# First stage of a two-layer kernel: k and v from one 512-column product, q from a 256-column one, and v copied ahead of q

## The reference, cut to what matters

```python
Q = _linear(query, Wq, bq)   # 16 heads of 16 features; query = layernorm(x)
K = _linear(key, Wk, bk)     # key = value = ctx
V = _linear(value, Wv, bv)
Qf = jnp.fft.rfft(Q, axis=2)
Kf = jnp.fft.rfft(K, axis=2)
corr = jnp.fft.irfft(Qf * jnp.conj(Kf), n=Lx, axis=2)
corr_mean = corr.mean(axis=-1)
top_w, top_idx = jax.lax.top_k(corr_mean, 4)
# softmax over the four, then V rolled by the four lags and summed
...
x = x + out @ Wo.T + bo
```

## Time and profile before

| | |
|---|---|
| device time, three executions | 984.47, 981.14, 981.69 us |
| their median | 981.69 us |
| span of the profiled execution, first to last instruction | 979.1 us |
| median less that span | 2.6 us |
| PE matmul busy / weight loads busy | 846.7 us (86%) / 544.5 us (56%) |
| DVE / ACT / POOL busy | 697.8 (71%) / 529.5 (54%) / 304.3 us (31%) |
| mean granted TensorE clock | 0.947 |

### The profile page before, as it was taken

How to read it: one execution, slowest core, us unless ns; L and a number is a source line. 1 busy time by engine, 2 the same in 40 slices (tenths; PEclk the granted TensorE clock), 3 DMA queues, 4 the chain that set the end, 5 groups by cost and what they waited for, 6 DMA issues and landing times.

```text
span 979.1 us, 13076 instructions
## 1 busy us (share of the span) xinstructions
PE 846.7 (86%) x4559; PEld 544.5 (56%) x4559; DVE 697.8 (71%) x1256; ACT 529.5 (54%) x1004; POOL 304.3 (31%) x236
## 2 busy tenths in 40 slices
PE   3999989699999999989999888799998997008998
PEld 3776766578677887434444444444443443006887
DVE  2466677866766577679879999767765998895333
ACT  1444443555333566677666777133336995983432
POOL 2100000466311122578868888310002331000000
PEclk9999999899999999999989999989998999558999
DMA  8800000010000000000000000000001435830111
GB/s 286 273 1 1 1 1 1 0 55 1 1 1 12 1 1 1 1 1 1 2 1 1 2 1 2 1 0 1 0 1 43 172 150 192 354 120 21 44 54 55
DMA packets 23448, 45.44 MB, mean 46 GB/s; under 512 B 2323, under 2 KB 18646, under 8 KB 22230
## 3 DMA queue, kind: packets, MB, share of 16 engines
q1 hardware_dynamic: 21776, 43.08, 12.3%
q10 hardware_dynamic: 1606, 1.52, 0.5%
HBM read 27.80 MB, written 16.78 MB: 46 GB/s over the span
## 4 chain that ended last, share of the span: by engine, by line
PE 64%; DVE 13%; ACT 9%; POOL 7%; issue 4%; DMA 1%; ACTq 1%; DVEq 0%; SPq 0%; POOLq 0%
PE pair L1307 9%; PE pair L1354 8%; PE pair L985 5%; PE pair L1223 5%; POOL hat L608 4%; PE pair L1238 4%; PE pair L1093 3%; PE pair L1120 3%; PE pair L989 3%; DVE wide L1812 3%; PE pair L1199 2%; PE pair L1030 2%; PE pair L1122 2%; ACT upq L917 2%; ACT g2q L923 2%
## 5 line engine op out<-in xcount | busy, mean ns | idle before, releaser
L608 POOL TENSOR_TENSOR hat<-hat 128x1024 f32<-128x1024 f32 x62 | 145.4, 2360 | 38.1 <-DVE hat L1663 38.0
L1332 PE MATMUL pair<-xqs,wuT 128*128 128x512 f32 x192 | 85.5, 606 | 4.8 <-ACT up_stage L873 4.8
L1307 PE MATMUL pair<-xqs,wgT 128*128 128x512 f32 x192 | 84.5, 597 | 0.0
L1354 PE MATMUL pair<-wdT,hid 128*128 128x256 f32 x384 | 83.1, 379 | 0.3 <-DVE hid L1860 0.3
L525 POOL TENSOR_TENSOR rstd<-lnt,half 128x8 f32<-128x8 f32 (+2 forms) x15 | 26.5, 1767 | 170.0 <-DVE lnt L1398 170.0
L1354 PEld LDWEIGHTS pair<-wdT,hid 128*128 128x128 f32 x384 | 72.9, 190 | 11.0 <-DVE hid L1860 1.2
L1207 PE MATMUL pair<-rows,sel 32*128 32x512 bf16 x256 | 68.3, 395 | 9.9 <-ACT down_a L828 2.9
L1223 PE MATMUL pair<-hat,vz 128*32 128x128 f32 x1056 | 71.6, 282 | 2.8 <-DVE hat L1663 1.6
L1223 PEld LDWEIGHTS pair<-hat,vz 128*32 128x32 f32 x1056 | 53.8, 112 | 25.7 <-issue 23.3
L1332 PEld LDWEIGHTS pair<-xqs,wuT 128*128 128x128 f32 x192 | 37.2, 195 | 51.8 <-issue 51.8
L985 PE MATMUL pair<-wT,ft_sb 128*128 128x256 f32 x256 | 64.4, 395 | 0.0
(11 more groups left out here) (223 smaller groups left out, 1931.0 us busy)
## 6 DMA issues: line engine op xcount, KB each, us to landing
up_far<-up_stage SPq DMA_DIRECT2D x24, 512.0 KB, 2.6
ups<-up_far SPq DMA_DIRECT2D x8, 1536.0 KB, 6.8
x_sb<-in_x_dram SPq DMA_DIRECT2D x8, 512.0 KB, 7.8
c_sb<-in_ctx_dram SPq DMA_DIRECT2D x8, 512.0 KB, 8.2
out_dram<-x_sb SPq DMA_DIRECT2D x16, 256.0 KB, 2.1
four<-in_c_four_dram SPq DMA_DIRECT2D x1, 1280.0 KB, 6.3
deq<-in_L_ffn_w_gate_dram SPq DMA_DIRECT2D x1, 768.0 KB, 6.9
deq<-in_L_ffn_w_up_dram SPq DMA_DIRECT2D x1, 768.0 KB, 8.6
```

The costliest lines, as they stand in the source:

```text
L608: nc.gpsimd.tensor_tensor(hat[:, n % RING, :], hat[:, (n - 2) % RING, :], hat[:, n % RING, :], ALU.add).then_inc(summed, 1)
L1307: last = mm(bank[2 + oc][:], wgT[:, c, oc * 128:(oc + 1) * 128], xqs[:, s, c, :], start=(c == 0), stop=(c == DC - 1))
L1332: last = mm(bank[2 + oc], wuT[:, c, oc * 128:(oc + 1) * 128], xqs[:, t % 2, c, :], start=(c == 0), stop=(c == DC - 1))
L1354: last = mm(bank[s][:, 0:D], hid[:, s, ic, :], wdT[:, ic, :], start=(ic == 0), stop=(ic == IC - 1))
```

## The change

In `project`, the product of q stands alone in `bank[2 + s]` with a bias of 256 columns. k and v now share `bank[4 + s]`: a bias of 512 columns and two products of 512 columns, whose moving operand is `wT[:, 1:3, c, :]`, two runs of 256 columns. In `copy_qv` the copy of v comes first and the three copies of q behind it; each still waits for `proj_done`, and the semaphores are raised by the same copies as before. `products` reads k from `bank[4 + s]`. `fold_half` waits for `prod_done` of all batches beside `v_copied`.

```diff
@@ copy_qv (ACT)
+                nc.scalar.activation(vhat[:, at(b), :].rearrange("p o d -> p (o d)"), bank[4 + s][:, D:], ACT.Copy).then_inc(v_copied, 1)
                 q = bank[2 + s][:, 0:D]
                 nc.scalar.activation(qq[:, s, 0, :], q, ACT.Copy)
                 nc.scalar.activation(qq[0:64, s, 1, :], q[64:128], ACT.Copy)
                 nc.scalar.activation(qq[64:128, s, 1, :], q[0:64], ACT.Copy).then_inc(q_copied, 1)
-                nc.scalar.activation(vhat[:, at(b), :].rearrange("p o d -> p (o d)"), bank[4 + s][:, 0:D], ACT.Copy).then_inc(v_copied, 1)
@@ project (PE)
-                mm(bank[2 + s][:], dc3, bias3[:, BAT["bq"]:BAT["bq"] + 2 * D], start=True, stop=False)
-                for i in range(2):
-                    for c in range(DC):
-                        mm(bank[2 + s][:, i * D:(i + 1) * D], ft_sb[:, s, i * DC + c, :], wT[:, i, c, :],
-                           start=False, stop=(i == 1 and c == DC - 1))
-                mm(bank[4 + s][:, 0:D], dc3, bias3[:, BAT["bv"]:BAT["bv"] + D], start=True, stop=False)
+                mm(bank[2 + s][:, 0:D], dc3, bias3[:, BAT["bq"]:BAT["bq"] + D], start=True, stop=False)
                 for c in range(DC):
-                    last = mm(bank[4 + s][:, 0:D], ft_sb[:, s, DC + c, :], wT[:, 2, c, :], start=False, stop=(c == DC - 1))
+                    mm(bank[2 + s][:, 0:D], ft_sb[:, s, c, :], wT[:, 0, c, :], start=False, stop=(c == DC - 1))
+                mm(bank[4 + s], dc3, bias3[:, BAT["bk"]:BAT["bk"] + 2 * D], start=True, stop=False)
+                for c in range(DC):
+                    last = mm(bank[4 + s].rearrange("p (i d) -> p i d", i=2), ft_sb[:, s, DC + c, :], wT[:, 1:3, c, :],
+                              start=False, stop=(c == DC - 1))
                 last.then_inc(proj_done, 1)
@@ fold_half (PE)
                     pe.wait_ge(v_copied, B)
+                    pe.wait_ge(prod_done, B)
@@ products (DVE)
-                k = bank[2 + s][:, D:2 * D]
+                k = bank[4 + s][:, 0:D]
```

## The result

The changed kernel is slower: its time is 1.0055 of the kernel before, 95% interval 1.0031 to 1.0080, which is +5.4 us (+3.0 to +7.9) on the median of 981.37 us of 22 executions. The forecast was +4.3. The profiled execution has a span of 985.5 us.

A forecast was written before the change was run, and what follows sets the result against it. The first stage was taken to begin bound by TensorE and end bound by a two-tick wait loop through ScalarE's q copies. Products -0.2 and copy order +4.5 gave +4.3 us on 981.69: 986.0 us, range 983.0 to 988.8.

The forecast's parts named there:

- Where and by what: Late first stage: a two-tick loop through ScalarE's copies of q sets the end, 10.1 us a turn.
- The products: In `project`, four merged 512-column records replace eight of 256: gain 0.01 us a batch, 0.2 us in all.
- The rule of 0.10 at the head of a run: TensorE fp32 runs: about 0.10 us once, then 0.2157 us per 256-column record; a 512-column record takes 0.429.
- The rival in which a 512-column record costs less than two of 256: TensorE's merged products: a cheaper 512-column record makes the kernel faster, about 978 us; chance 0.04.
- The size of the delay: First stage: later `q_copied` costs 4.5 to 5.0 us, 4.5 taken; floor 3.57 us.
- the copies' distance: ScalarE in `copy_qv`: copies start 0.397 us apart, so `q_copied` comes 0.397 us later in every batch.
- the same recurrence: Delay carried over 28 ticks, 34 to 166 us, less the slack of xn: 4.1 to 4.6 us at the last `transform`.
- The number of turns: First stage: the chain of waits goes through ScalarE's copies of q nine times, each paying 0.397 us.
- After the stage: From 175 us on all work follows the chain; nothing takes the shift back, so it passes on whole.
- one more fall behind a longer wait there: Rival: in the first stage a longer wait for xn drops the clock again, 988 to 990 us; chance 0.10.
- the sum of 4.3: Whole kernel: products -0.2 and order of copies +4.5 us make +4.3 us.
- The weight loads' wait for xn: First stage, `transform` on TensorE: the wait for xn should grow from 10.7 us by some 4.

The follow-up runs named there:

- the double delay: Kernel before with ScalarE copying v twice ahead of q, once into an unread scratch tile: executions took 993.1 to 1011.6 us, no ratio.
- the single one: Kernel before with only ScalarE's copy of v moved ahead of the three copies of q: 1.0040 (1.0006 to 1.0073), +3.9 us.

## Why the prediction was right, and where it was not

**Where and by what: right.** The late part of the stage turns in a loop of two ticks through ScalarE's copies of q, and the copy of v was put into that loop. Turns of 10.12, 10.40 and 10.67 us for zero, one and two copies, and 10.12 again with the changed products and no copy ahead, show it.

**The products: right.** 0.01 us a tick and 0.2 us in the stage were forecast. Three ticks went from 13.21 to 13.18 us and the stage without the delay from 149.0 to 148.8. The rule of 0.10 at the head of a run and 0.2157 or 0.429 for each record held for the new run (0.463 measured, 0.462 by the rule). The rival in which a 512-column record costs less than two of 256 is out.

**The size of the delay: mis-sized.** The step that failed is the copies' distance. The prediction took 0.397 us from the three intervals of the earlier trace rows and gave it to the copy of v at its new place. In all three a copy of half the partitions, which reads 64 rows and writes the other 64, stands before or behind. Two whole copies in a row are 0.28 us apart (39.18 to 39.46), as v and the next `copy_ft` were before. What was added to the loop is the distance at the new place, and that is 0.28. With it the same recurrence gives 3.3 us where 4.5 stood, and the stage, with the estimate for the clock, shows 2.6.

**The number of turns: nearly.** Nine were counted, ten came; the recurrence's remark that paths close behind the chain grow was borne out by the double delay (6.5 us in the stage, where nine turns at 0.56 ask for 5.0); at the single one it read 0.7 us too much, for the stage's 2.6 us are what nine or ten turns at 0.28 ask for.

**After the stage: a term was missing.** The step "I see nothing that takes the shift back" let the shift pass to the end as it is. It passes, but the clock behind it is another: in the profiled executions 0.74 us of shift at 481.64 became 6.82 at 606.24, by two falls of the clock. A plain delay of 2.6 us at the start measured +5.1 (+1.2 to +9.0) with clocks from 0.931 to 0.949, one of 5.1 us +3.1 (+0.2 to +6.1) with clocks from 0.949 up. The prediction had weighed the clock only within the stage (one more fall behind a longer wait there), at a tenth; the profiled execution lost none there, and lost it in the sampling (0.95 to 0.92). That the sum of 4.3 came near to 5.4 is in part luck, two errors of opposite sign: 1.7 us too much in the stage, and the later clock left out.

**The weight loads' wait for xn** grew from 10.7 to 22.4 us in the waits of the stage, where "some 4" was forecast:

```profile
PEld pair L967 <- DVE xn L1409: 22.4, 23, 2.8
```

With the copies reordered and the old products it is 13.8 us in 16 waits, 3.1 more. The rest belongs to the changed products: behind a record of 512 columns the next weight load comes 0.41 us ahead of its matmul (38.57 and 38.98), so it begins to wait earlier. It costs the matmuls nothing: they waited for xn 8.4 us in the changed kernel and 8.3 with the old products and v first, 11 times each.

```profile
PE pair L967 <- DVE xn L1409: 8.4, 11, 2.0
```

```profile
PE pair L967 <- DVE xn L1409: 8.3, 11, 2.0
```

**What stays open.** How much of the 5.4 us the later clock takes is known only as the remainder, some 2.8 us, between 0.4 and 5.3 by the interval; by the medians of all 22 executions, 8.2 us apart, it would be some 5.6. The 6.1 us above are those of one execution. Why nearly all executions of the kernel before have one and the same clock, and why a few microseconds of delay spread them, isn't shown by these runs.

## What to carry to other kernels

An engine that is busy 41% of a stretch can still set its time, when its instructions stand in a loop of waits between two other engines; the chain of waits shows the loop, and the time of a turn is the number to watch. Give each product that somebody waits for its own semaphore: the three edits that did it here took the delay out or gained 7 to 11 us, where the merged product had 0.2 to give. Take the distance of two instructions from a pair of the same kind in the same order, since the distance depends on the neighbour and not on the instruction alone. When a small change moves the time by another amount than its stage, follow one recurring instruction through both profiles: the place where the shift jumps is where to look.

## What was not expected of the hardware

- Copies on ScalarE of 384, 381 and 376 ns each started 0.28 us apart when both were whole 128-partition copies, and 0.39 to 0.41 us apart when one of the two moved 64 partitions to the other 64.
- One fall of the clock in the sampling made a step of 17.60 us take 21.79 and made what follows that much later; between such falls the same work stayed 2.6 us late from 503 to 588 us.
- A delay of 0.9 to 5.1 us ahead of unchanged work left executions with mean granted clocks anywhere from 0.931 to 0.953, where 21 of 23 without it lay between 0.946 and 0.951. A difference of 0.3% between two such kernels is to be read together with their clocks.
